# A four-layer graph network: attention tops and first-convolution flags in PSUM, nine one-hot columns in the second convolution, edge lines gathered in two stages

## The chip, the cores and the metric

The kernel runs on one core of one Trainium2 chip. The metric is device time in microseconds (us) of one execution. Engines are named as in the profile: PE (matmuls; PEld its weight loads), DVE, ACT, POOL, and SP, which issues transfers.

## The reference

6250 nodes carry 16 features. 206,250 edges are sorted by destination. Four layers follow one another, each as x + layer(relu(layernorm(x))):

```python
edge_index = jnp.stack([src, dst])
h = relu(layernorm(x)); x = x + gcn(h, edge_index, ...)           # first convolution
h = relu(layernorm(x)); x = x + nnconv(h, edge_attr_6, ...)       # second convolution
h = relu(layernorm(x)); x = x + sheaf(h, edge_index, ...)         # sheaf layer
h = relu(layernorm(x)); x = x + attention(h, edge_attr_16, ...)   # attention
```

- The first convolution sums normalised features of the source over each destination's edges: `segment_sum(h[src] * norm, dst)`.
- The second makes a 16x16 matrix of each edge's six attributes by a small network, multiplies the source's features by it, and takes the mean over the destination's edges.
- The sheaf layer makes two reflections (Householder matrices) for each edge from the features at its ends and sums messages at both ends.
- Attention makes 256 logits for each edge: `e2 = w_a * feat[src]` with `w_a = efeat @ W_attn + b_attn` as 16x16. `seg_max = segment_max(e2, dst)`, `ex = exp(e2 - seg_max[dst])`, and the output is the sum over edges of `e1 * ex / denom`, with `denom` the sum of `ex`.

## The kernel before

Edges lie on 128 partitions, 1612 in a row on each. The first three layers go through them in 62 blocks of 26 edge columns; attention groups edges of one destination in quads of four and goes through 440 quads a partition in 110 blocks of four quads. Between layers a node stage (`node_sums`) collects each destination's sum and norms. Each engine has its own program, written by hand; the engines wait for one another's semaphore counts, and the order of work on an engine is the order of its code. `At` is a block's place, `walk` unrolls some first and last blocks and loops over the rest two at a time, and `Chain` counts DVE's completions: `ch.do` counts one, `ch.to` and `ch.sync` wait for those so far, `ch.tell` waits and then signals another engine.

**Features of sources.** Part of the source rows comes by gather: POOL issues one indirect transfer for each edge column (`gather`, lines L1168, L1479, `sources` L1954, L2494). The rest comes by PE, from a table in weights: DVE or ACT makes one-hot rows (`hot`, L1191, L1610, L1687) from the source's key, PE multiplies them by the table's pieces (`summed`), DVE keeps the one wanted block of the sum (`mask`, which writes `held`), PE turns it (`picked`) and ACT copies it on (`moved`). In the first convolution this is three groups of four columns with seven one-hot rows each, all on DVE; in the second it is two groups of four columns, seven rows on ACT for one of them and four on ACT, three on DVE for the other. 14 columns of the first convolution and 18 of the second are gathered. In the second, `matrices` makes the edge's weights `w` on PE, `times` (L1711) multiplies by the features and `total` (L1719) adds up.

**Sums by destination.** A scan along each row (`scan_block`, L688) adds messages, with flags that reset it where a destination begins. In the first convolution `high_digits` (L238) and `low_digits` make one-hot digits from which PE counts degrees on the side.

**Quads and lines.** `put_quads` (L909, in the head of the second convolution, on POOL) writes where the quads begin. The node stage behind the second convolution (`quads_of_edges`, DVE) fills in which edges are in each quad, and marks void places. A line is what attention needs of the edges of a quad. For half of the quads POOL gathers lines in the sheaf layer, four each in 55 blocks (`lines` L1963), DVE puts in the void marks (`fixed` L2204) and POOL adds to the ids (`ids_of` L1971); SP stores them. The other half is gathered in attention (L2505).

**Sheaf.** Each block is done in two halves: DVE turns the gathered features (`turned`, L2257), PE and ACT make vectors from them, ACT squares, DVE multiplies (L2271) and widens (L2320), and PE sums.

**Attention.** For block `at`, DVE finds quad maxima in two steps (`larger`, L2695), carries maxima along the row (`forward` L2702) and back (`back` L2707), all in the tile `S`, subtracts them (`below` L2712), and multiplies ACT's exponentials by the messages (`product` L2719). `drop` (L2743) and `carried` (L2753) prepare the sum that enters from the block before. Between these stand the `times` (L2680) of the next block, which multiply PE's `w` in PSUM by gathered features. PE's `quad_sum` adds each quad into one of two banks `pq`, and ACT's `put_state` (L2624) copies the bank into `S`:

```python
to = pq[q % 2].rearrange("p (t c) -> p t c", t=2)
turn_wait(e, s_prod, at.of(QB, q + 1))
turn_wait(e, s_state, at.of(QB, q + 1))
for n in range(4):
    e.matmul(to, ident[:, :], X[:, q, :, n, :], start=n == 0, stop=False)
```

## Time and profile before

| | us |
|---|---|
| median of 3 runs (9060.18 to 9061.02) | 9060.25 |
| profiled execution | 9049.36 |
| its span | 9047.6 |
| first convolution, 120 to 1330 | 1210 |
| second convolution, 1470 to 3020 | 1550 |
| node stage and norm, 3020 to 3260 | 240 |
| sheaf, 3260 to 5810 | 2550 |
| attention, 5900 to 8930 | 3030 |
| busy over the span: PE / DVE / ACT / POOL | 7287.6 / 7667.6 / 4453.0 / 6665.2 |

The span is what the profiler recorded of one execution, from the first instruction to the last; the profiled execution's time has 1.8 us around it and lies 10.9 us below the median of the timed runs. The stretches of the stages were cut by hand where the lines of one stage end and those of the next begin. Busy time leaves out the issue of transfers, which on POOL takes 0.30 us ahead of each gather.

### The profile page before, as it was taken

To read this page: it belongs to the slowest core of one execution; us is meant where nothing else is said; L and a number is where in the kernel's file an instruction comes from. 1 tells how busy PE (TensorE), PEld (TensorE's weight loads), DVE (VectorE), ACT (ScalarE), POOL (GpSimd) and SP (SyncE) were. 2 spreads that over 40 slices of the span, in tenths; PEclk is the share of its full clock that TensorE was granted. 3 is DMA by queue.
4 is the path that set the end of the run, shared out by engine and by line. 5 is a ranking of instruction groups with operands and counts; after the bars stand their busy time and mean duration, and the time that the engine had idled before them with its cause. 6 is when DMAs were issued, how large, how long until landed. Compare 5 with 4: busy or idle time off the path is not lost. (4 is left out here: it accounts for less than half of the span.)

```text
span 9047.6 us, 135625 instructions
## 1 busy us (share of the span) xinstructions
PE 7287.6 (81%) x35152; PEld 4135.0 (46%) x35152; DVE 7667.6 (85%) x11882; ACT 4453.0 (49%) x7248; POOL 6665.2 (74%) x6335
## 2 busy tenths in 40 slices
PE   3778765888888258888888889578888888888884
PEld 2666653555555135555555555323333333333331
DVE  7999984777777468888888888589999999999997
ACT  4666664666666146666665556323333333333333
POOL 5777777777777577777777777377777777777774
PEclk9888886888888579999999999789999999999997
DMA  4222221112111111111111111122222222222223
GB/s 148 59 59 59 59 53 35 44 45 46 45 44 45 20 24 32 28 32 29 31 29 31 28 32 20 16 62 80 75 75 81 76 75 75 82 75 75 76 81 98
DMA packets 499695, 493.19 MB, mean 55 GB/s; under 512 B 181075, under 2 KB 396906, under 8 KB 498731
## 3 DMA queue, kind: packets, MB, share of 16 engines
q1 hardware_dynamic: 299595, 371.60, 12.2%
q0 software_dynamic: 199904, 119.78, 9.7%
q14 instruction: 171, 1.40, 0.0%
q8 instruction: 25, 0.41, 0.0%
HBM read 240.96 MB, written 249.95 MB: 54 GB/s over the span
## 5 line engine op out<-in xcount | busy, mean ns | idle before, releaser
L2494 POOL DMA_INDIRECT attn_got<-tab,attn_line x1760 | 2111.3, 1200 | 582.6 <-issue 499.4
L1954 POOL DMA_INDIRECT sheaf_got<-tab,sheaf_idx x1612 | 1710.3, 1061 | 490.0 <-issue 474.0
L2547 PE MATMUL attn_q<-attn_X,ident 128*128 128x512 f32 x3520 | 1743.8, 635 | 3.3 <-DVE attn_X L2719 1.8
L2043 PE MATMUL sheaf_acc<-sheaf_hot_hi,sheaf_wide 128*128 128x392 bf16 x6696 | 1356.9, 345 | 279.5 <-DVE sheaf_hot_hi L2246 276.1
L1479 POOL DMA_INDIRECT nnconv_got<-tab,nnconv_idx x1116 | 1082.0, 970 | 402.1 <-issue 335.1
L2547 PEld LDWEIGHTS attn_q<-attn_X,ident 128*128 128x128 f32 x3520 | 678.2, 204 | 1085.7 <-issue 1085.7
L1168 POOL DMA_INDIRECT gcn_got<-tab,gcn_idx x868 | 901.8, 1039 | 317.9 <-issue 279.2
L2680 DVE TENSOR_TENSOR attn_T<-attn_w,attn_got 128x1024 f32<-128x1024 f32 x880 | 1034.8, 1217 | 79.6 <-DVE attn_T L2712 34.1
L2043 PEld LDWEIGHTS sheaf_acc<-sheaf_hot_hi,sheaf_wide 128*128 128x128 bf16 x6696 | 656.4, 106 | 816.5 <-issue 488.4
L2624 ACT COPY attn_S<-attn_q 128x512 f32<-128x512 f32 x440 | 255.9, 582 | 1559.8 <-PE attn_q L2556 1559.8
L1257 PE MATMUL gcn_acc<-gcn_hot,pieces 128*128 128x512 f32 x2604 | 752.3, 448 | 268.7 <-DVE gcn_hot L1191 267.2
L1191 DVE SCALAR_TENSOR_TENSOR gcn_hot<-gcn_key,key_of,gcn_one 128x512 fp32r<-128x512 f16 x1302 | 872.3, 740 | 4.6 <-DMA gcn_blk<-src_blk 4.6
L2538 PE MATMUL attn_w<-src_hi 32*128 32x512 f32 x3520 | 588.4, 741 | 342.8 <-DVE attn_T L2680 341.9
L1257 PEld LDWEIGHTS gcn_acc<-gcn_hot,pieces 128*128 128x128 f32 x2604 | 554.3, 219 | 402.5 <-issue 280.7
L1711 DVE TENSOR_TENSOR nnconv_prod<-nnconv_w,nnconv_got 128x1024 f32<-128x1024 f32 x434 | 490.3, 1142 | 271.4 <-PE nnconv_w L1514 270.7
L2043 PE MATMUL sheaf_acc<-sheaf_hot_act,sheaf_wide 128*128 128x392 bf16 x2976 | 613.6, 345 | 0.0
L2105 ACT ACTIVATE sheaf_zT<-sheaf_z,sheaf_b 128x832 f32<-128x832 f32 x248 | 223.2, 951 | 722.3 <-PE sheaf_z L1995 722.3
L2712 DVE SCALAR_TENSOR_TENSOR attn_T<-attn_T,attn_S 128x1024 f32<-128x1024 f32 x440 | 536.0, 1218 | 17.3 <-DVE src_lo L2743 16.6
L1514 PE MATMUL nnconv_w<-nnconv_W,nnconv_tT 64*128 64x256 f32 x3224 | 537.3, 462 | 4.4 <-DVE nnconv_prod L1711 4.4
L1529 PE MATMUL nnconv_acc<-nnconv_hot,pieces 128*128 128x512 f32 x1736 | 529.5, 465 | 11.7 <-ACT nnconv_hot L1610 11.7
L2719 DVE SCALAR_TENSOR_TENSOR attn_X<-attn_T,attn_X 128x1024 f32<-128x1024 f32 x440 | 525.8, 1215 | 1.2 <-ACT attn_X L2610 1.2
L2246 DVE TENSOR_SCALAR sheaf_hot_hi<-sheaf_number,src_hi 128x784 bf16<-128x784 f16 x1116 | 477.9, 428 | 42.8 <-PE sheaf_acc L2043 26.2
(503 smaller groups left out, 13356.6 us busy)
## 6 DMA issues: line engine op xcount, KB each, us to landing
sums<-attn_S SPq DMA_DIRECT2D x110, 1024.0 KB, 4.2
tops<-attn_S SPq DMA_DIRECT2D x110, 512.0 KB, 3.0
attn_got<-tab,attn_line POOLq DMA_INDIRECT x1760, 2.5
sheaf_got<-tab,sheaf_idx POOLq DMA_INDIRECT x1612, 2.5
gcn_key<-src_key SPq DMA_DIRECT2D x62, 384.0 KB, 3.7
gcn_blk<-src_blk SPq DMA_DIRECT2D x62, 384.0 KB, 4.2
nnconv_got<-tab,nnconv_idx POOLq DMA_INDIRECT x1116
nnconv_key<-src_key SPq DMA_DIRECT2D x62, 256.0 KB
```

The source lines that it names most:

```text
L1168: e.indirect_dma_start(out=got[at.b][:, j, :], out_offset=None, in_=tab[0], in_offset=indices(idx[at.b], j)).then_inc(s_got[at.b], 16)
L1191: hit = e.scalar_tensor_tensor(out=hot[q][:, n, :], in0=key[at.b][:, g, :], scalar=key_of[:, n:n + 1], in1=pone[:, :], op0=ALU.is_equal, o ...
L1257: mm = e.matmul(pacc[q][:, :], pieces[:, part, n * NBLK:(n + 1) * NBLK, :].rearrange("p b f -> p (b f)"), hot[q][:, n, :], start=n + part ...
L1479: e.indirect_dma_start(out=got[at.b][:, j, :], out_offset=None, in_=tab[1], in_offset=indices(idx[at.b], j)).then_inc(s_got_of[part][at.b] ...
L1514: mm = [e.matmul(to[:, t * 512 + (j - 2 * g) * 256:t * 512 + (j - 2 * g + 1) * 256], tT[at.b][t * H1:(t + 1) * H1, j * P:(j + 1) * P], W2[ ...
L1954: e.indirect_dma_start(out=got[at.b][:, j, D:D + T2], out_offset=None, in_=tab[2], in_offset=indices(idx[at.b], j)).then_inc(s_got[half][a ...
L2043: mm = e.matmul(pacc[k][:, 0:HH], wide[at.b][half][:, part, col, :], hot[:, k * HH:(k + 1) * HH], start=False, stop=False, skip_group_chec ...
L2494: e.indirect_dma_start(out=got[at.b][:, 4 * q + n, :], out_offset=None, in_=tab[3], in_offset=indices(ids[:, q, n, :], D + 2)).then_inc(s_ ...
L2538: e.matmul(pw[n // 2][:, n % 2 * 512:(n % 2 + 1) * 512], efT[at.b][n * RW:(n + 1) * RW, q, :], Wc[n * RW:(n + 1) * RW, :], start=True, sto ...
L2547: e.matmul(to, ident[:, :], X[:, q, :, n, :], start=n == 0, stop=False)
L2680: e.tensor_tensor(T[at.b][:, q, :, 2 * half:2 * half + 2, :].rearrange("p t n (i o) -> p n t i o", o=D), pw[half].rearrange("p (n t i o) - ...
L2712: return ch.do(e.scalar_tensor_tensor(out=Tb[:, q, 0, :, :], in0=Tb[:, q, 0, :, :], scalar=1.0, in1=Sb[:, q, None, 0:CH].to_broadcast([P, ...
```

## The change

First convolution: the scan's flags, and a table of digits for `high_digits`, lie in PSUM; the ones that the hot rows read shrink to 128 columns; the seventh one-hot row of each group goes from DVE to ACT, as Square and Relu (`last_row`). Second convolution: three groups of three columns in place of two of four, so 17 columns are gathered; rows on ACT are 7, 5 and 0 of seven, the rest on DVE; masks stand ahead of the totals. From block 14 on, two lines a block are gathered there too, 96 in all, with index and marks on ACT and ids on DVE. `quads_of_edges` moves from the node stage into blocks 10 to 13, in pieces, and `void_src` goes. Sheaf: two lines a block in all 62 blocks in place of four in 55; the ids are added on DVE. Attention: the tops lie in PSUM (`ptop`), which ACT copies out (`tops_out`); `pq` shrinks to one bank; `times` come in halves between the steps of the maxima, and some waits of DVE for its own completions go.

```diff
@@ first convolution
-            runT, msgT, flags = ([sbl(f"{n}{b}", [P, D, J + 1]) for b in range(2)] for n in ("runT", "msgT", "flags"))
+            runT, msgT = ([sbl(f"{n}{b}", [P, D, J + 1]) for b in range(2)] for n in ("runT", "msgT"))
+            pflag = [ps(f"gcn_flag{b}", [P, 512], banks) for b in range(2)]
+            flags = [t[:, 0:D * (J + 1)].rearrange("p (f j) -> p f j", f=D) for t in pflag]
+            high = pone[:, P:P + C]
+            BY_DVE = NC - 1
-                        for n in range(NC):
-                            hit = e.scalar_tensor_tensor(out=hot[q][:, n, :], in0=key[at.b][:, g, :], scalar=key_of[:, n:n + 1],
-                                                         in1=pone[:, :], op0=ALU.is_equal, op1=ALU.mult)
+                        for n in range(BY_DVE):
+                            hit = e.scalar_tensor_tensor(out=hot[q][:, n, :].rearrange("p (j m) -> p j m", j=GW),
...
+                                                         in1=pone[:, None, 0:P].to_broadcast([P, GW, P]), op0=ALU.is_equal, op1=ALU.mult)
+                    def last_row(at, g):
+
+                        q = (at.b * GP + g) % 2
+                        if g == 0:
+                            e.wait_ge(s_rows[at.b], at.half(32, 32))
+                        e.wait_ge(s_acc, at.of(GP, g + 1))
+                        e.activation(hot[q][:, NC - 1, :], key[at.b][:, g, :], ACT.Square,
+                                     bias=key_neg[:, NC - 1:NC]).then_inc(s_apart, 1)
+                        e.wait_ge(s_apart, at.of(GP, g + 1))
+                        e.activation(hot[q][:, NC - 1, :], hot[q].bitcast(F32)[:, NC - 1, :], ACT.Relu, scale=-1.0,
+                                     bias=ones[:, 0:1]).then_inc(s_last, 1)
@@ second convolution
-        GN = 2
-        BY_ACT = (NC, 4)
+        GN, GC = 3, 3
+        BY_ACT = (NC, 5, 0)
+                    def lines(ln):
+
+                        turn_wait(e, s_at, ln.of(1, 1))
+                        if ln.k >= 2:
+                            turn_wait(e, s_lst[ln.b], ln.half(16, 0))
+                        for q in range(NP2):
+                            e.indirect_dma_start(out=line[ln.b][:, q, :, :].rearrange("p n f -> p (n f)"), out_offset=None,
+                                                 in_=a["lines"], in_offset=indices(line_at[ln.b], q)).then_inc(s_ln[ln.b], 16)
...
+                        if at.k >= KL:
+                            lines(at.plus(-KL))
...
+                            if more and pair[0] in (2, 4):
+                                mask(at.plus(1), pair[0] // 2)
                             for g in pair:
                                 added[g] = total(at, g)
-                            if more and pair[0] == 2:
-                                mask(at.plus(1), 1)
+                            if at.k == KL - 3 and pair[0] == 0:
+                                quads_across()
+                            if at.k == KL - 2 and pair[0] == 0:
+                                quads_carried()
+                            if more and pair[0] == 0:
+                                chosen(at.plus(1), 2)
...
+                        if at.k == KL - 4:
+                            quads_within()
+                        if at.k == KL - 2:
+                            quads_of_edges()
+                        if at.k == KL - 1:
+                            quads_joined()
+                        if at.k >= KL:
+                            ids_of(at.plus(-KL))
@@ sheaf, POOL
                     def step(at):
                         sources(at, 0)
-                        if 0 < at.k <= NBL:
-                            ids_of(at.plus(-1))
                         sources(at, 1)
-                        if at.k < NBL:
-                            lines(at)
+                        lines(at)
@@ attention
-            pq = [ps(f"attn_q{q}", [P, 512], banks) for q in range(2)]
+            pq = ps("attn_q", [P, 512], banks)
+            ptop = ps("attn_tops", [P, QB * CH], banks).rearrange("p (q c) -> p q c", q=QB)
-                        turn_wait(e, s_state, at.of(QB, q + 1))
+                        turn_wait(e, s_state, at.of(QB, q + 2))
+                    def tops_out(at):
+
+                        e.wait_ge(s_sub, at.of(QB, QB))
+                        e.copy(S[at.b][:, :, 0:CH], ptop).then_inc(s_copied, 1)
-                                out=Sb[:, q, 0:CH], in0=Sb[:, q + 1, 0:CH], scalar=apart_q[:, bass.ds(at.of(QB, q + 1), 1)],
+                                out=ptop[:, q, :], in0=ptop[:, q + 1, :], scalar=apart_q[:, bass.ds(at.of(QB, q + 1), 1)],
-                        ch.tell(s_top)
+                        e.scalar_tensor_tensor(out=drop[:, :], in0=So[:, QB - 1, 0:CH], scalar=1.0, in1=ptop[:, 0, :],
+                                               op0=ALU.mult, op1=ALU.subtract).then_inc(s_top, 1)
                         below(0)
-                        ch.tell(s_sub)
```

Three places show what moves. On ACT in the first convolution, from the store of one block's run (`gcn_run`) on, there stood before:

```order
L1328 COPY gcn_run<-gcn_runT 128x416
L1306 COPY gcn_msgT<-gcn_sel 128x4x16
L692 COPY gcn_flags<-same 128x16x26
L1335 ACTIVATE gcn_apart<-iota_f,src_lo 128x128 x8
L1306 COPY gcn_msgT<-gcn_sel 128x4x16
L1335 ACTIVATE gcn_apart<-iota_f,src_lo 128x128 x9
```

and now stands:

```order
L1251 COPY gcn_run<-gcn_runT 128x416
L1218 ACTIVATE gcn_hot<-gcn_key,key_neg 128x512
L1221 ACTIVATE gcn_hot<-gcn_hot,ones 128x512
L1235 COPY gcn_msgT<-gcn_got 128x14x16
L1239 COPY gcn_idx<-srci 128x14
L1229 COPY gcn_msgT<-gcn_sel 128x4x16
L695 COPY gcn_flag<-same 128x16x26
L1258 ACTIVATE gcn_apart<-iota_f,src_lo 128x128 x8
L1218 ACTIVATE gcn_hot<-gcn_key,key_neg 128x512
L1221 ACTIVATE gcn_hot<-gcn_hot,ones 128x512
L1229 COPY gcn_msgT<-gcn_sel 128x4x16
L1258 ACTIVATE gcn_apart<-iota_f,src_lo 128x128 x9
```

A Square and a Relu (`gcn_hot`) come ahead of each copy of a group's sums (`gcn_msgT<-gcn_sel`, which is `moved`), and the copies of gathered rows and of the next indices come to the start of the step.

On DVE in the second convolution, in the products (`nnconv_prod`, which is `times`) and totals (`nnconv_msgT`) of one block, there stood before:

```order
L1711 TENSOR_TENSOR nnconv_prod<-nnconv_w,nnconv_got 128x1024 x2
L1719 TENSOR_REDUCE nnconv_msgT<-nnconv_prod 128x4x16 x2
L1711 TENSOR_TENSOR nnconv_prod<-nnconv_w,nnconv_got 128x1024 x2
L1719 TENSOR_REDUCE nnconv_msgT<-nnconv_prod 128x4x16 x2
L1695 SCALAR_TENSOR_TENSOR nnconv_held<-nnconv_blk,blk_of,nnconv_acc 128x512
L1711 TENSOR_TENSOR nnconv_prod<-nnconv_w,nnconv_got 128x1024 x2
L1719 TENSOR_REDUCE nnconv_msgT<-nnconv_prod 128x4x16 x2
L1687 TENSOR_SCALAR nnconv_hot<-nnconv_key,key_of 128x512 x3
```

and now stands:

```order
L1724 TENSOR_TENSOR nnconv_prod<-nnconv_w,nnconv_got 128x1024 x2
L1732 TENSOR_REDUCE nnconv_msgT<-nnconv_prod 128x4x16 x2
L1700 TENSOR_SCALAR nnconv_hot<-nnconv_key,key_of 128x384 x7
L1724 TENSOR_TENSOR nnconv_prod<-nnconv_w,nnconv_got 128x1024 x2
L1708 SCALAR_TENSOR_TENSOR nnconv_held<-nnconv_blk,blk_of,nnconv_acc 128x384
L1732 TENSOR_REDUCE nnconv_msgT<-nnconv_prod 128x4x16 x2
L1724 TENSOR_TENSOR nnconv_prod<-nnconv_w,nnconv_got 128x1024 x2
L1708 SCALAR_TENSOR_TENSOR nnconv_held<-nnconv_blk,blk_of,nnconv_acc 128x384
L1732 TENSOR_REDUCE nnconv_msgT<-nnconv_prod 128x4x16 x2
L1700 TENSOR_SCALAR nnconv_hot<-nnconv_key,key_of 128x384 x2
```

The mask of the next block's group (`nnconv_held`) has moved ahead of two totals, there is one mask more, and nine one-hot rows of 384 columns stand in place of three of 512.

On DVE in attention, from the quad maxima (`attn_two`) of one block on, there stood before:

```order
L2695 SCALAR_TENSOR_TENSOR attn_two<-attn_T 128x2048
L2695 SCALAR_TENSOR_TENSOR attn_S<-attn_two 128x4x256
L2702 SCALAR_TENSOR_TENSOR attn_S<-attn_S,apart_q 128x256
L2691 SCALAR_TENSOR_TENSOR attn_line<-void,attn_line 128x8
L2680 TENSOR_TENSOR attn_T<-attn_w,attn_got 128x2x2x256 x2
L2702 SCALAR_TENSOR_TENSOR attn_S<-attn_S,apart_q 128x256 x3
L2707 SCALAR_TENSOR_TENSOR attn_S<-attn_S,apart_q 128x256
L2712 SCALAR_TENSOR_TENSOR attn_T<-attn_T,attn_S 128x1024
```

and now stands:

```order
L2798 SCALAR_TENSOR_TENSOR attn_two<-attn_T 128x1024 x2
L2783 TENSOR_TENSOR attn_T<-attn_w,attn_got 128x2x2x256
L2798 SCALAR_TENSOR_TENSOR attn_S<-attn_two 128x4x256
L2794 SCALAR_TENSOR_TENSOR attn_line<-void,attn_line 128x8
L2805 SCALAR_TENSOR_TENSOR attn_S<-attn_S,apart_q 128x256
L2783 TENSOR_TENSOR attn_T<-attn_w,attn_got 128x2x2x256
L2805 SCALAR_TENSOR_TENSOR attn_S<-attn_S,apart_q 128x256
L2783 TENSOR_TENSOR attn_T<-attn_w,attn_got 128x2x2x256
L2805 SCALAR_TENSOR_TENSOR attn_S<-attn_S,apart_q 128x256
L2805 SCALAR_TENSOR_TENSOR attn_tops<-attn_S,apart_q 128x256
L2811 SCALAR_TENSOR_TENSOR attn_tops<-attn_tops,apart_q,attn_S 128x256
L2816 SCALAR_TENSOR_TENSOR attn_T<-attn_T,attn_tops 128x1024
```

Halves of the next block's products (`attn_T<-attn_w`) stand between `larger` and the steps of `forward`, and from the last of these on the tops are written to and read from PSUM (`attn_tops`).

## Rows read from the trace of the kernel before

**Rows 1.** Windows, attention: us, busy of PE, PEld, DVE, ACT, POOL; clock; DMA.

```profile
5900.00:8930.00 3030.00, 2681.64 (x8343) 1054.14 (x8343) 2863.43 (x3079) 970.19 (x1865) 2323.18 (x1970) 0.93 0.26 76
```

**Rows 2.** Timeline of DVE, first convolution: start, us, operation, xcount [idle before <-releaser].

```profile
700.68 1.06 DVE L688 TENSOR_TENSOR_SCAN gcn_runT<-gcn_flags,gcn_msgT 128x432 f32<-128x432 f32 x1
...
702.71 4.69 DVE L1191 SCALAR_TENSOR_TENSOR gcn_hot<-gcn_key,key_of,gcn_one 128x512 fp32r<-128x512 f16 x7
...
707.32 1.48 DVE L238 TENSOR_TENSOR gcn_digits<-iota_b,src_hi 128x1274 bf16<-128x1274 bf16 x1
...
719.73 1.06 DVE L688 TENSOR_TENSOR_SCAN gcn_runT<-gcn_flags,gcn_msgT 128x432 f32<-128x432 f32 x1
```

**Rows 3.** Timeline of POOL, the same stretch.

```profile
700.93 1.57 POOL L1168 DMA_INDIRECT gcn_got<-tab,gcn_idx  x1 [0.30 <-issue]
...
707.84 1.78 POOL L1168 DMA_INDIRECT gcn_got<-tab,gcn_idx  x1 [0.30 <-issue]
...
711.18 0.95 POOL L1168 DMA_INDIRECT gcn_got<-tab,gcn_idx  x1 [0.30 <-issue]
```

**Rows 4.** Waits of ACT, first convolution: us in total, times, longest.

```profile
ACT gcn_msgT L1306 <- PE gcn_sel L1269: 391.4, 125, 18.5
```

**Rows 5.** Timeline of POOL, second convolution, the first gathers of three blocks.

```profile
1668.49 1.01 POOL L1479 DMA_INDIRECT nnconv_got<-tab,nnconv_idx  x1 [0.99 <-POOL nnconv_idx L1473]
...
2432.74 0.97 POOL L1479 DMA_INDIRECT nnconv_got<-tab,nnconv_idx  x1 [0.96 <-POOL nnconv_idx L1473]
...
2955.82 0.97 POOL L1479 DMA_INDIRECT nnconv_got<-tab,nnconv_idx  x1 [1.85 <-DVE nnconv_prod L1711]
```

**Rows 6.** Waits of DVE and of PE, second convolution.

```profile
DVE nnconv_prod L1711 <- PE nnconv_w L1514: 270.7, 131, 3.3
...
PE nnconv_sel L1542 <- DVE nnconv_held L1695: 187.5, 99, 2.7
```

**Rows 7.** Timeline of DVE, sheaf, two transposes in the last blocks.

```profile
5579.34 0.60 DVE L2257 STREAM_TRANSPOSE sheaf_gT<-sheaf_got 128x416 f32<-128x416 f32 x1
...
5599.70 0.60 DVE L2257 STREAM_TRANSPOSE sheaf_gT<-sheaf_got 128x416 f32<-128x416 f32 x1
```

**Rows 8.** Waits of DVE, sheaf.

```profile
DVE sheaf_line L2204 <- issue: 82.2, 24, 3.6
```

**Rows 9.** Waits of DVE, attention.

```profile
DVE attn_T L2680 <- DVE attn_T L2712: 34.1, 109, 0.3
...
DVE attn_T L2712 <- DVE src_lo L2743: 16.6, 105, 0.2
```

**Rows 10.** Groups of POOL, attention: busy us, mean ns | idle before <-releasers.

```profile
L2494 POOL DMA_INDIRECT attn_got<-tab,attn_line x1752 | 2103.7, 1201 | 580.1 <-issue 497.0 <-DMA attn_line<-quad_lines 58.0 <-DMA attn_got<-tab,attn_line 16.5
```

**Rows 11.** Groups by form of ACT, second convolution.

```profile
L1606 ACT ACTIVATE nnconv_hot<-nnconv_key,key_neg 128x512 fp32r<-128x512 f16 x671 | 424.1, 715 | 0.0
```

**Rows 12.** Groups by form of PEld (weight loads), second convolution.

```profile
L1529 PEld LDWEIGHTS nnconv_acc<-nnconv_hot,pieces 128*128 128x128 f32 x1730 | 384.5, 229 | 151.6 <-issue 62.8
```

**Rows 13.** Groups by form of POOL, node stage behind the second convolution.

```profile
L880 POOL DMA_INDIRECT agg<-runs,last_edge x49 | 52.1, 1063 | 14.9 <-issue 14.9
```

**Rows 14.** Timeline of ACT, attention.

```profile
7514.40 0.59 ACT L2624 COPY attn_S<-attn_q 128x512 f32<-128x512 f32 x1 [3.52 <-PE attn_q L2556]
```

**Rows 15.** Timeline of PE, attention.

```profile
7514.29 1.14 PE L2538 MATMUL attn_w<-src_hi 32*128 32x512 f32 x8
...
7529.07 2.09 PE L2538 MATMUL attn_w<-src_hi 32*128 32x512 f32 x8 [3.15 <-DVE attn_T L2680]
```

**Rows 16.** Timeline of DVE, attention.

```profile
7515.69 2.34 DVE L2680 TENSOR_TENSOR attn_T<-attn_w,attn_got 128x1024 f32<-128x1024 f32 x2
```

**Rows 17.** Groups by form of DVE, attention.

```profile
L2680 DVE TENSOR_TENSOR attn_T<-attn_w,attn_got 128x1024 f32<-128x1024 f32 x880 | 1034.8, 1217 | 79.6 <-DVE attn_T L2712 34.1 <-DVE attn_X L2719 29.2 <-PE attn_w L2538 8.8
...
L2712 DVE SCALAR_TENSOR_TENSOR attn_T<-attn_T,attn_S 128x1024 f32<-128x1024 f32 x440 | 536.0, 1218 | 17.3 <-DVE src_lo L2743 16.6
...
L2753 DVE SCALAR_TENSOR_TENSOR src_lo<-attn_S,src_lo 128x512 f32<-128x512 f32 x110 | 75.4, 686 | 0.0
```

More of the change, by code:

```diff
@@ L1359, in _ @@
                     flagged(At(0))
+                    for g in range(GP):
+                        last_row(At(0), g)
                     for g in range(GP - 1):
+                        last_row(At(1), g)
                         moved(At(0), g)
@@ L1574, in _ @@
                     summed(At(1), 0)
-                    walk(e, NB, step)
+                    walk(e, NB, step, head=KL)
                 @block.scalar
@@ L1719, in total, with quads_within @@
                         return ch.do(e.tensor_reduce(by_edge(msgT[at.b][:, :, 1 + 4 * g:1 + 4 * g + n]), prod[g % 3][:, 0:n, :, :], AX.X, ALU.add))
+                    def quads_within():
+                        ch.do(e.memset(nil[:, :], 0.0))
+                        ch.do(e.memset(moved_on[:, 0:1], 0.0))
+                        e.wait_ge(s_pool, 2)
+                        ch.do(e.tensor_copy(edge_f[:, :], edge_i[:, :]))
+                        ch.do(e.tensor_copy(f4[:, :], lane_i[:, :]))
+                        e.wait_ge(s_ld, 32)
+                        flags = begun[:, :, 3]
+                        ch.do(e.tensor_scalar(goes[:, :], flags, -1.0, 1.0, ALU.mult, ALU.add))
+                        ch.do(e.tensor_reduce(f1[:, :], flags, AX.X, ALU.add))
+                        ch.sync()
+                        for f in range(3):
+                            ch.do(e.tensor_tensor_scan(fill[:, f, :], goes[:, :], begun[:, :, f], 0.0, ALU.mult, ALU.add))
+                        ch.do(e.tensor_scalar(f1[:, :], f1[:, :], 0.5, None, ALU.is_lt))
+                        ch.sync()
+                        ch.do(e.tensor_copy(ends[:, :], fill[:, :, LQ - 1]))
+                        ch.do(e.tensor_scalar(diag[:, :], ident[:, :], f1[:, 0:1], None, ALU.mult))
+                        ch.tell(s_end)
@@ L1721, in step, with ids_of @@
+                    def ids_of(ln):
+                        e.wait_ge(s_ln[ln.b], ln.half(16 * NP2, 16 * NP2))
+                        ids = line[ln.b].bitcast(I32)[:, :, :, D + 2]
+                        e.scalar_tensor_tensor(out=ids, in0=void[:, bass.ds(ln.of(QB, 0), NP2), :], scalar=float(NP), in1=ids,
+                                               op0=ALU.mult, op1=ALU.add).then_inc(s_ids, 1)
                     def step(at):
@@ L2669, in _, with times @@
                     e.sem_inc(s_t, 2)
-                    def times(at, q):
-                        if q == 0 and at.k >= 2:
+                    def times(at, q, halves=(0, 1)):
+                        if q == 0 and at.k >= 2 and 0 in halves:
                             e.wait_ge(s_prod, at.of(QB, -QB))
-                        if q % 2 == 0:
+                        if q % 2 == 0 and 0 in halves:
                             e.wait_ge(s_got[q // 2][at.b], at.half(16 * EH, 16 * EH))
-                        for half in range(2):
+                        for half in halves:
                             for n in (2 * half, 2 * half + 1):
```

425 lines of the change are left out of this document (228 added, 197 removed).

## The prediction

> **What bounds the kernel now.** I read the table of windows by stage first; its row for attention [rows 1] shows DVE busy for 2863 of 3030 us and POOL for 2323, to which POOL's issue gaps come. Neither is the one full engine of the program: the stages have different limits, so each is read by itself, in its timelines and then its waits, for what ends last there.
>
> First convolution, 62 blocks. In DVE's timeline the scans of two blocks start at 700.68 and 719.73 [rows 2]: 19.05 us a block. DVE fills it with 21 one-hot rows (seven in 4.69, a new one every 0.66), three masks, `high_digits` (1.48) and the scan (1.06). POOL needs as long: 14 gathers of 0.95 with 0.30 between, but the one that starts in `high_digits` takes 1.78 and the one that starts in the scan 1.57 [rows 3]; both end about 0.8 after the DVE instruction does. Those two read both inputs from SBUF. The hot rows, whose ones lie in PSUM, delay no gather. ACT waits 391 us for PE's sums, 6.3 a block [rows 4]: it has room.
>
> Second convolution, 62 blocks. POOL starts block 8 at 1668.49, block 40 at 2432.74 and block 61 at 2955.82 [rows 5]. To block 40 that is 23.9 a block, the gaps before a block being only those behind its index copy; after it 24.9, with waits of about 2 for DVE's products. POOL falls back in the head, where it also puts out quad rows, regains its lead in 32 blocks and then waits. So the consumers bound, at 24.9: DVE waits 270.7 for PE's `w`, PE 187.5 for DVE's masks [rows 6], of which `mask(1)` stands behind two totals.
>
> Sheaf, 62 blocks of 41 us (2550 / 62). POOL's 26 sources and 4 lines take 37.5 even undisturbed and its gathers never stop in the loop, which looks like a bound. Against it: the last seven blocks gather no lines, and there two halves still start 20.4 apart, 5579.34 and 5599.70 [rows 7]. Also DVE stops 24 times for 3.4 at the line copy, once a turn of the loop, for nothing that the profile shows [rows 8].
>
> Attention, 110 blocks of 27.5 (3030 / 110). DVE waits mostly for its own dependent steps, 0.16 to 0.32 each [rows 9]. POOL's gathers average 1.20 instead of 0.95 [rows 10].
>
> **The change part by part.**
>
> First convolution. DVE loses three rows, 2.0: 17.1. POOL loses the two delays, 0.83 + 0.62: 14 x 1.25 = 17.5. ACT gains three rows, each a Square of 128x512, 0.72 in the second convolution [rows 11], and a Relu of the same 512 elements that depends on it and that I price alike: 1.4 a row, 4.2 a block, on 19.05 - 6.3 = 12.8: 17.0. Three engines within half a microsecond, with ACT's rows queued ahead of `moved`, will not interlock perfectly. I take 18.0: -1.05 x 62 = **-65**. Ends: 17.5 (-96), and ACT taking it all back (0).
>
> Second convolution. POOL gives up one of 18 gathers a block (-1.25) and takes two line gathers (+2.5) in the last 48: about 22.7 before block 14 and 25.2 after it, and perhaps 0.2 for nine DVE rows in place of three. DVE turns 3 rows and 2 masks into 9 and 3 shorter ones: at 0.66 for 512 columns [rows 2] and 0.5 for 384, 5 x 0.66 = 3.3 becomes 12 x 0.5 = 6.0, at most +2.7. It also takes over the edge-of-quad work, some 40 instructions on 440 columns: at half of a scan's 1.06, 20 us in four blocks. PE goes from 28 products to 42: no more columns to speak of, but 14 more weight loads of 0.229 [rows 12], so 0 to +3.2; I take +1.3. What pays: masks come before totals, so PE's 3.0 a block for them shrinks, and DVE's wait for `w` behind it. I let both cancel. POOL's 25.2 to 25.4 against 24.9 then eats its regained lead over 48 blocks without becoming the bound for long. With the 20 us, partly in DVE's waits for PE, and a little for POOL at the end: **+20**. Ends: 0 (POOL's own sum: -62 x 1.25 + 96 x 1.25 = +43, less the 2 us waits of 20 blocks) and +100 (consumers +1.3 a block).
>
> Node stage behind it. Its 49 gathers are the path: 52.1 + 14.9 [rows 13]. At 0.945 they would take 46.3; the edge-of-quad instructions beside them go: **-4**, between -6 and 0.
>
> Sheaf. POOL loses two lines and two small additions a block, 3.0 of 41; DVE exchanges a copy for an addition of the same size. By the tail POOL is not what ends last: **-5**. Ends 0, and -105 if 1.7 of POOL's 3.0 a block came off (the other 1.3 standing for the stop of 3.4 in every second block).
>
> Attention. On DVE the wait after `below(0)` goes (0.3), that after `drop` (0.16), `forward` steps lie between halves of `times` (0.2), `larger` no longer waits for all of `two` (0.1), and `carried` tells without a wait: 0.7 to 1.0 a block, cover included. POOL loses what `below`, `back` and part of `forward` held: of 16 x 0.26 = 4.1 a block I expect 1.6 to go, which leaves POOL below DVE. In the way stands PE. `quad_sum(1)` writes the one bank that `put_state(0)` still reads, so it waits for that copy (0.59 [rows 14]) and two hand-overs, 0.8. The `w` behind it now ends at 7514.29 + 1.14 = 7515.43, and DVE begins with it at 7515.69 [rows 15, 16]: a slack of 0.26. So up to half a microsecond comes back as a wait there. Later in the block PE waits 3.15 for DVE, and the eight matmuls behind that wait take 2.09 instead of 1.14; so the 0.8 has room only in the 3.15. Half of the pure gain of 1.0 lost would be -55, none lost -110; I take -0.7 x 110 = **-77**, ends 0 and -115.
>
> Does a PSUM operand cost DVE more? `times`, with one input in PSUM, takes 1.217 and `below`, all SBUF, 1.218 for the same 1024 elements [rows 17]. A hot row of 512 with its ones in PSUM takes 4.69 - 6 x 0.66 = 0.73, `carried` of 512 in SBUF 0.686. So 0 to 0.05 an instruction; I take 0. The Trainium skill, "VectorE: DVE Perf Modes", section "The TRN2 errata — SBUF-src ops pay a fixed extra latency per instruction", lists a fixed 58 cycles for SBUF and 120 for PSUM, which makes an estimate of 0.065 us for each of nine instructions that move in an attention block: by that the sum would lose 64 us. The rows of 1024 elements do not agree with it, those of 512 nearly do.
>
> Sum: -65 + 20 - 4 - 5 - 77 = -131. The profiled execution took 9049.4, its span 9047.6; so 8918. The median of the three runs lies 10.9 above that execution: **8929 us**.
>
> **Rivals.**
> - *ACT becomes the first convolution's bound*, 19 a block: Square and Relu stand between PE's sum and `moved` in its order. For it the thin margin, against it 6.3 of idle for 4.2 of work. No gain there: 8994. Chance 0.13.
> - *The single bank costs attention its gain*: DVE waits for `w` as long as PE for the copy, -0.1 x 110 instead of -77: 8995. For it the slack of 0.26, against it the idle 3.15. Chance 0.14.
> - *PSUM operands are dearer*: nine instructions at 0.05 in 110 blocks, 50, and two in 62 blocks, 6: 8985. Chance 0.10.
> - *Sheaf was bound by POOL after all*: -105 instead of -5: 8829. For it POOL's unbroken row, against it the tail. Chance 0.10.
> - *The second convolution's added work lies on its path*, the slower side: PE and DVE already wait for each other, so +1.3 and +2.7 add up: 62 x 4.0 = 248 instead of 20: 9157. It decides from (131 + 20) / 62 = 2.4 a block on. Against it the 3.0 a block that PE now waits for masks. Chance 0.08.
>
> **How the numbers follow.** The forecast has 0.45, the rivals 0.55. Sheaf's -105 and the slower case are left out (0.18). The rest spans 8845, with the first convolution and attention at their best ends (8929 - 31 - 38, and some from sheaf), to 9040, with one rival of the middle group and the second convolution at +65. As the forecast's own range I see 8875 to 8985. 0.2% is 18 us, about what a measurement of this kernel can tell from no change: faster 0.83, same 0.07, slower 0.10.
>
> **What would show it.** First convolution: scans 17.5 to 18.3 apart, gathers all near 0.95, ACT with little idle time. Second: gathers 25.2 a block at the end, PE's wait for masks below 100 in all, blocks near 25. Sheaf: POOL waiting for DVE, blocks still near 41. Attention: gathers near 1.10, a new wait of PE for `attn_S` of about 0.8 a block, DVE waiting 0.2 to 0.5 for `w`. The prediction is wrong if the second convolution's blocks pass 26, if the first stays at 19, or if DVE's wait for `w` in attention reaches 1 a block.

## The result and the profile after

The changed kernel takes **9259.57 us** (median of 4 runs, 9256.27 to 9261.85), the kernel before 9060.22: a ratio of 1.022, 95% interval 1.0203 to 1.0238. It is slower by 199 us, where 131 less was forecast, and outside the predicted range.

The profiled execution has a span of 9260.1 us against 9047.6. Here is where the 212.5 us between them lie. A stage's length is taken on VectorE, from the first start to the last of its one-hot rows, its products, its transposes and its maxima (`gcn_hot`, `nnconv_prod`, `sheaf_gT`, `attn_two`), from the listing of one tile's instructions:

| stage | before | after | difference | forecast |
|---|---|---|---|---|
| first convolution | 1177.8 | 1081.6 | -96 | -65 |
| from it to the second | 185.0 | 197.2 | +12 | 0 |
| second convolution | 1523.6 | 1752.0 | +228 | +20 |
| node stage | 211.7 | 207.0 | -5 | -4 |
| sheaf | 2517.3 | 2589.7 | +72 | -5 |
| attention | 2978.9 | 2978.0 | -1 | -77 |

The rows add up to 210; the rest lies ahead of the first stage, between the sheaf layer and attention, and behind attention.

The table of windows after, one row a stage; the last answers to [rows 1] (us; busy time and count on PE, PEld, DVE, ACT, POOL; granted clock of PE, where 1.00 is the upper of its two levels, 2.4 GHz, and 0.50 the lower, 1.2 GHz; DMA):

```profile
120.00:1230.00 1110.00, 921.20 (x5678) 774.13 (x5678) 1020.68 (x1493) 1044.09 (x2455) 825.75 (x868) 0.90 0.25 62
1385.00:3160.00 1775.00, 1381.19 (x7910) 1108.71 (x7909) 1359.70 (x1885) 943.23 (x1686) 1131.86 (x1212) 0.84 0.19 47
3365.00:5960.00 2595.00, 2291.37 (x13713) 1368.08 (x13714) 2138.63 (x5252) 1508.88 (x1646) 1827.20 (x1713) 0.90 0.14 23
6110.00:9140.00 3030.00, 2655.97 (x8341) 1021.64 (x8341) 2833.65 (x3189) 1071.69 (x1975) 2135.42 (x1971) 0.95 0.26 76
```

No engine is full in the second convolution: the longest, PE and DVE, are busy for 1381 and 1360 of 1775 us. They wait for each other, and for longer than in [rows 6]:

```profile
PE nnconv_sel L1518 <- DVE nnconv_held L1708: 362.3, 175, 6.0
DVE nnconv_prod L1724 <- PE nnconv_w L1489: 351.9, 131, 5.9
```

In the sheaf layer DVE still waits for nothing that the profile shows where it did in [rows 8], and in a second place, both 24 times, once a turn of the loop:

```profile
DVE sheaf_line L2300 <- issue: 80.1, 24, 3.5
DVE sheaf_prod L2369 <- issue: 33.6, 24, 1.6
```

In attention DVE is busy 30 us less and POOL's gathers are shorter (1099 ns against 1201 in [rows 10]), but the time stays; the group of `times`, whose wait for PE's `w` was 8.8 in [rows 17], and PE's wait for the copy out of the one bank:

```profile
L2783 DVE TENSOR_TENSOR attn_T<-attn_w,attn_got 128x1024 f32<-128x1024 f32 x880 | 1054.4, 1220 | 151.7 <-PE attn_w L2637 116.5 <-DVE attn_X L2823 29.5 <-DMA attn_got<-tab,attn_line 5.6
```
```profile
PE attn_q L2646 <- ACT attn_S L2726: 91.8, 114, 0.9
```

### The profile page after: what moved, and what is told of

It reads as the page before. It is cut to its first block and busy times, and to the rows that moved or that the text cites. A ratio compares the mean times of both kernels' runs of the same rounds, so it can differ in the third digit from the quotient of the medians.

```text
span 9260.1 us, 138201 instructions
## 1 busy us (share of the span) xinstructions
PE 7358.3 (79%) x36144; PEld 4337.8 (47%) x36144; DVE 7636.0 (82%) x12309; ACT 4727.1 (51%) x8012; POOL 6324.6 (68%) x6163
## 5 line engine op out<-in xcount | busy, mean ns | idle before, releaser
L2593 POOL DMA_INDIRECT attn_got<-tab,attn_line x1760 | 1933.9, 1099 | 770.5 <-issue 502.6
L2140 PE MATMUL sheaf_acc<-sheaf_hot_hi,sheaf_wide 128*128 128x392 bf16 x6696 | 1412.0, 355 | 286.4 <-DVE sheaf_hot_hi L2344 286.4
L1452 POOL DMA_INDIRECT nnconv_got<-tab,nnconv_idx x1054 | 1018.8, 967 | 386.1 <-issue 297.0
L2646 PEld LDWEIGHTS attn_q<-attn_X,ident 128*128 128x128 f32 x3520 | 651.7, 198 | 1191.7 <-issue 1191.7
L2783 DVE TENSOR_TENSOR attn_T<-attn_w,attn_got 128x1024 f32<-128x1024 f32 x880 | 1054.4, 1220 | 151.7 <-PE attn_w L2637 116.5
L1073 POOL DMA_INDIRECT gcn_got<-tab,gcn_idx x868 | 825.8, 951 | 303.8 <-issue 276.2
L1097 DVE SCALAR_TENSOR_TENSOR gcn_hot<-gcn_key,key_of,gcn_one 128x512 fp32r<-128x512 f16 x1116 | 750.4, 743 | 4.0 <-DMA gcn_blk<-src_blk 4.0
L1505 PE MATMUL nnconv_acc<-nnconv_hot,pieces 128*128 128x384 f32 x2604 | 700.0, 438 | 16.5 <-ACT nnconv_hot L1600 9.9
L2140 PE MATMUL sheaf_acc<-sheaf_hot_act,sheaf_wide 128*128 128x392 bf16 x2976 | 656.6, 363 | 0.0
L1505 PEld LDWEIGHTS nnconv_acc<-nnconv_hot,pieces 128*128 128x128 f32 x2604 | 643.7, 264 | 18.6 <-issue 18.6
L2816 DVE SCALAR_TENSOR_TENSOR attn_T<-attn_T,attn_tops 128x1024 f32<-128x1024 f32 x440 | 533.0, 1211 | 0.0
```

Source lines behind the costliest of these rows:

```text
L1073: e.indirect_dma_start(out=got[at.b][:, j, :], out_offset=None, in_=tab[0], in_offset=indices(idx[at.b], j)).then_inc(s_got[at.b], 16)
L1097: hit = e.scalar_tensor_tensor(out=hot[q][:, n, :].rearrange("p (j m) -> p j m", j=GW), in0=key[at.b][:, g, :].rearrange("p (j m) -> p j m ...
L1452: e.indirect_dma_start(out=got[at.b][:, j, :], out_offset=None, in_=tab[1], in_offset=indices(idx[at.b], j)).then_inc(s_got_of[part][at.b] ...
L1505: mm = e.matmul(pacc[:, 0:GC * P], pieces[:, part, n * NBLK:(n + 1) * NBLK, :].rearrange("p b f -> p (b f)"), hot[q][:, n, :], start=n + p ...
L2140: mm = e.matmul(pacc[k][:, 0:HH], wide[at.b][half][:, part, col, :], hot[:, k * HH:(k + 1) * HH], start=False, stop=False, skip_group_chec ...
L2593: e.indirect_dma_start(out=got[at.b][:, 4 * q + n, :], out_offset=None, in_=tab[3], in_offset=indices(ids[:, q, n, :], D + 2)).then_inc(s_ ...
```

## The experiments

The chips on which they ran timed the kernel before at 9048.8 to 9068.8 us (medians), so single times are read beside the kernel before on the same chip, and small differences by the stage's length. That has a spread too: with its code as it was before, sheaf takes 2509.0 to 2522.7 us in five runs, attention 2978.9 to 2991.5 in three.

### Second convolution: the masks' place

The timelines of DVE and of PE in the kernel after, block 30 or so (start, us, operation, xcount, idle before):

```profile
2304.93 2.34 DVE L1732 TENSOR_REDUCE nnconv_msgT<-nnconv_prod 128x64 f32<-128x1024 f32 x2
2307.18 2.41 DVE L1700 TENSOR_SCALAR nnconv_hot<-nnconv_key,key_of 128x384 fp32r<-128x384 f16 x7
2309.51 2.34 DVE L1724 TENSOR_TENSOR nnconv_prod<-nnconv_w,nnconv_got 128x1024 f32<-128x1024 f32 x2
2311.78 0.60 DVE L1708 SCALAR_TENSOR_TENSOR nnconv_held<-nnconv_blk,blk_of,nnconv_acc 128x384 f32<-128x384 f16 x1
2312.30 2.33 DVE L1732 TENSOR_REDUCE nnconv_msgT<-nnconv_prod 128x64 f32<-128x1024 f32 x2
2318.90 1.23 DVE L1724 TENSOR_TENSOR nnconv_prod<-nnconv_w,nnconv_got 128x1024 f32<-128x1024 f32 x1 [4.26 <-PE nnconv_w L1489]
```
```profile
2303.71 2.73 PE L1505 MATMUL nnconv_acc<-nnconv_hot,pieces 128*128 128x384 f32 x14
...
2308.32 1.14 PE L1489 MATMUL nnconv_w<-nnconv_W,nnconv_tT 64*128 64x256 f32 x8
2312.68 1.12 PE L1518 MATMUL nnconv_sel<-nnconv_pick,nnconv_held 128*128 128x32 f32 x6 [3.21 <-DVE nnconv_held L1708]
2313.61 4.00 PE L1505 MATMUL nnconv_acc<-nnconv_hot,pieces 128*128 128x384 f32 x14
```

PE's sum is complete at 2306.4. By then DVE is in two totals, and its program has seven one-hot rows and two products before the mask, which starts 5.3 us after the sum, at 2311.78. PE waits 3.21, its next sum takes 4.00 instead of 2.73, and DVE, which ran ahead to the mask, waits 4.26 for the `w` behind that sum. Each engine's delay is the other's next wait. The wait also costs clock: in the windows of PE the granted clock is 1.00 during the first sum (2303.7 to 2306.4), and 0.50 from 2313.5 to 2315.5 in the sum behind the wait, which is what makes the same 14 matmuls longer.

**Masks early.** In `step` of DVE (changed kernel), the mask that PE waits for goes ahead of what does not need it:

```diff
-                            if more and pair[0] in (2, 4):
-                                mask(at.plus(1), pair[0] // 2)
                             for g in pair:
                                 added[g] = total(at, g)
...
+                            if more and pair[0] in (0, 2):
+                                mask(at.plus(1), pair[0] // 2 + 1)
                             if more and pair[0] == 0:
                                 chosen(at.plus(1), 2)
```

> The changed kernel with two of VectorE's masks in the second convolution put earlier: the second mask behind the first pair's sums and ahead of its seven one-hot rows, the third behind the second pair's sums and ahead of the next products. Theory (order: the masks stand behind products and rows that do not need them, and TensorE waits for them): TensorE's wait for the mask falls from 358.7 us to under 120, the later blocks from 28.2 to 24.7 to 25.7 us, the stage by 120 to 190 us, the time to 9070 to 9140. Rival (the ninth columns' work, the loads and the line gathers fill the block): the waits move to other names, the blocks stay at 27 or more, the time stays at 9210 to 9260.

Measured: 9035.7 us beside 9056.0 for the kernel before; the stage takes 1530.0 instead of 1752.0, a larger gain than I expected. DVE's wait for `w` nearly goes, and one for PE's sum, 17.8 in the changed kernel, comes:

```profile
PE nnconv_sel L1518 <- DVE nnconv_held L1708: 187.3, 60, 8.4
DVE nnconv_prod L1724 <- PE nnconv_w L1489: 50.1, 60, 5.1
DVE nnconv_held L1708 <- PE nnconv_acc L1505: 90.6, 60, 7.2
```

PE's wait did not fall below the 120 us that I expected: it is now one stop of about 3 us a block. That stop is not free: the sum behind it is again at the lower clock (granted 0.59 from 2202.4 to 2206.6) and takes 4.1 to 4.2 us, and DVE waits for it, 60 times and 90.6 us in all. But DVE waits for PE for 141 us in all, where it waited 370 in the changed kernel, and is busy for 1365 of the 1565 us between 1385 and 2950. The stage's 222 us come from the order alone, with the same instructions; how much of them is the clock (0.89 in this stage, 0.84 before the masks moved) and how much the waits themselves, no run separates. The rival falls.

**No lines.** The changed kernel, masks late, without the line gathers, index copies, marks and ids of this stage.

> The changed kernel, its masks where the change put them, without the line gathers of the second convolution and what goes with them on the other engines; half of the quads keep lines of zeros, so only the second convolution is read. Theory (the masks' place is the cost, the lines a little beside it): later blocks 27.2 to 27.6 us instead of 28.2, the stage 30 to 45 us shorter. Rival (the lines are the cost): blocks of 24.5 to 25.5 us, the stage 130 us shorter or more.

Measured: 1726.1 us, 26 less than the changed kernel and a little less of a gain than I expected: the lines cost little where the masks set the pace. (Its time was 9154.7, because the sheaf stage fell too, to 2508.8; see below.)

**Nine columns alone.** The kernel before with the three groups of three and the masks early; lines and quads' setup stay where they were.

> The kernel before with the nine columns in three groups in the second convolution alone, VectorE's masks early, and neither the edge lines nor the quads' setup in it. Theory (the columns themselves are a gain, their order took it): blocks of 23.0 to 23.7 us instead of 24.65, 60 to 100 us less, time 8950 to 9000. Rival (the second one-hot rows on VectorE and the third mask eat what eight or nine gathers less give): blocks of 24.4 to 25.0, time 9040 to 9080.

Measured: 8996.3 beside 9055.1; the stage takes 1465.9, 58 less than before. Blocks take 23.3 to 24.7 us, a little more than I expected, but the columns are a gain. Beside the run with masks early, 1530.0, lines and quads' setup in this stage cost 64 us together.

### First convolution: which part pays

Tiles lie in one of two memories on the chip, SBUF or PSUM; PE's sums go to PSUM.

**First convolution alone**, put into the kernel before.

> The kernel before with the change's first convolution alone. Theory (each stage's part stands by itself): first convolution's block 17.5 us, 95 us less, time 8955 to 8975. Rival (part of the stage's gain comes back where the next stages wait for transfers that start earlier): 8985 to 9030.

Measured: 8958.0 beside 9056.0, the stage 1079.6: this part stands by itself. **The seventh row back on VectorE** (changed kernel):

```diff
-            BY_DVE = NC - 1
+            BY_DVE = NC
```

> The changed kernel with the first convolution's seventh one-hot row back on VectorE. Theory (VectorE's sum of 19.05 us bounded the block of before, and the row's 2 us a block is the gain): blocks of 18.8 to 19.2 us instead of 17.5, 75 to 105 us more, time 9335 to 9365. Rival (the flags in the other memory, which make GpSimd's gathers cheaper, are the gain): blocks of 17.5 to 18.0, 0 to 30 us more.

**Flags and block numbers back in SBUF** (changed kernel):

```diff
-            flags = [t[:, 0:D * (J + 1)].rearrange("p (f j) -> p f j", f=D) for t in pflag]
-            high = pone[:, P:P + C]
+            flags = [sbl(f"flags{b}", [P, D, J + 1]) for b in range(2)]
+            high = sbl("high", [P, C])[:, :]
```

> The changed kernel with the first convolution's flags and the row of block numbers in SBUF as before, the seventh row on ScalarE. Theory (the seventh row on ScalarE is nearly all of the stage's gain): first convolution 0 to 30 us longer than the changed kernel's 1081 us. Rival (the flags in PSUM take VectorE out of the way of GpSimd's gathers, which bounded the block): 50 to 95 us longer.

Measured (VectorE is the profile's DVE): 1157.4 us with the row on VectorE and 1144.6 with the flags in SBUF, against 1081.6 with both parts and 1177.8 with neither. Each part alone gives 20 or 33 us, both together 96. Neither of my two expectations held as a whole: the row's holds in its size (76 back), but its time, 9232.6, does not, as the sheaf stage fell with it (see below); and the flags are not a small thing beside it (63 back, the rival's size; time 9325.7). They are two bounds of nearly the same length, and the stage keeps the one that is left: with the row on VectorE DVE is busy for 1072.8 of the 1100 us from 120 to 1220, with the flags in SBUF for 976.0, and there POOL's gathers (837.8) and their issue (257.5) fill the time. The listings of POOL's gathers show the second bound (min/median/max in ns), first of the changed kernel, then with the flags in SBUF:

```profile
L1073 POOL DMA_INDIRECT gcn_got<-tab,gcn_idx x868: 946/952/968, 124.2 to 1226.4; - x174
```
```profile
L1072 POOL DMA_INDIRECT gcn_got<-tab,gcn_idx x868: 947/952/2317, 123.8 to 1292.9; - x174
```

With the second inputs of the scan and of `high_digits` in PSUM no gather is longer than 968 ns; with both inputs in SBUF the longest takes 2317, 102 of the 868 take over 1200, and all together take 894.8 us instead of 825.8: 69 more, on a stage that is 63 longer. The Trainium skill says in "SBUF — State Buffer", section "Who interferes with whom", that a VectorE instruction with two inputs in SBUF contends with a GpSimd instruction that reads SBUF; the gathers take their indices from a tile there, and these two runs agree with it.

### Sheaf: what the 72 us are

My first theory was pace: POOL, with four line gathers a block before, held the halves at 19.4 us, and with two it no longer does. Two runs were to show it from both sides.

**Two spare line gathers** more in each block of the changed kernel, into tiles that nobody reads:

```diff
...
+                        for q in range(NP2):
+                            e.indirect_dma_start(out=spare[at.b][:, q, :, :].rearrange("p n f -> p (n f)"), out_offset=None,
+                                                 in_=a["lines"], in_offset=indices(edges_of, q)).then_inc(s_sp[at.b], 16)
...
```

> The changed kernel with two more line gathers a block in the sheaf layer, into tiles that nobody reads, so that GpSimd has its four line gathers a block again. Theory (GpSimd's gathers paced the halves of before; without them VectorE's and ScalarE's hand-overs meet badly): sheaf blocks of 40.8 to 41.4 us instead of 42.6, stage 70 to 100 us shorter, time 9160 to 9190. Rival (VectorE's two operations for the lines' ids and the stop at the loop's turn are the cost): blocks stay at 42.4 to 42.8 or get longer, time 9250 or more.

**Two lines less** in each block of the kernel before.

> The kernel before with two of the four line gathers a block left out of the sheaf layer; half of the quads keep lines of zeros, so attention works on other indices and only the sheaf stage is read. Theory (pacing): sheaf blocks grow from 41.0 to about 42.6 us, the stage by 70 to 100 us. Rival (GpSimd's gathers bound the block): blocks of 39 us or less, the stage 100 us shorter or more.

Measured: 2586.1 us with the spare gathers (2589.7 without), and 2505.0 with two lines less in the kernel before (2517.3). The theory falls on both sides. The rival of the second run falls as well: two gathers of about 1.25 less a block, 155 us of POOL's work, took at most 12 us off, about the spread of this stage, so POOL is no bound of it.

What spoke instead were two runs that had not touched the sheaf layer. With the seventh row on VectorE its stage took 2497.3, without lines in the second convolution 2508.8. Both changed the number of instructions ahead of the loop in VectorE's program, and with it the stops: both gone in the first (first instruction 2010), the second gone in the other (1985). **The program moved** tests that alone: the changed kernel with 18 tiny memsets at the stage's start, which put the loop's first instruction at VectorE's number 2010, where it is with the seventh row, instead of 1992.

```diff
                     ch.tell(s_ready)
+                    for n in range(18):
+                        ch.do(e.memset(prod[:, n % 13, n // 13, 0:1], 0.0))
```

> The changed kernel with 18 tiny memsets ahead of the sheaf loop in VectorE's program, so that the loop's first instruction is VectorE's number 2010, as in the run with the seventh row on VectorE, instead of 1992. Theory (the sheaf layer's 72 us are stops in which VectorE waits for instructions, and these hang on where its loop lies in its program): both stops at the loop's turn go, sheaf blocks 40.8 to 41.1 us, stage 80 to 95 us shorter, time 9160 to 9185. Rival (the stage's time hangs on ScalarE's program or on what the stage meets when it starts): blocks stay at 42.67, time 9245 or more.

Measured: 9174.9, the stage 2505.6, 84 us less for 18 instructions more. DVE's list of waits has neither stop any longer. The page's rows of the instruction queue, of the changed kernel and of this one (packets, MB):

```profile
q14 instruction: 184, 1.50, 0.1%
```
```profile
q14 instruction: 63, 0.52, 0.0%
```

121 packets less, five for each of 24 turns. Between 3600 and 5500 us, inside the loop, the changed kernel has 111 of them, the moved one none, and the kernel before, with one stop, 110: the packets go with the loop, but not with the second stop. I read it so: with the loop at 1992 VectorE has to fetch in each turn of its 370 instructions, with the loop at 2010 it does not. The transposes show what that did to a turn of two blocks. Without stops its four halves take 20.3 to 20.6 us (medians). With the first stop alone, in the kernel before, the half that holds it takes 22.2, but two others 19.4 and 19.8: the loop catches up. With both, 23.4, 20.5, 20.5 and 20.9: it does not. Why not is open; no run has the second stop alone.

**48 and 176 memsets** in the kernel of all parts that pay (below) were to show which places are good.

> The parts that pay, together, with 48 tiny memsets ahead of the sheaf loop, so that the loop begins at VectorE's instruction 1370 instead of 1322. 2010, where no stop was seen, is 1370 and five times 128. If the place that matters repeats every 128 instructions, the stop of 3.5 us at the loop's turn goes and the sheaf stage takes 2495 to 2508 us instead of 2516. If it repeats every 256, this place lies half a period off 2010 and the stop can stay. Rival (the place in the whole program or another engine's decides): the stop stays here and with 176.

> The same with 176 memsets: the loop begins at VectorE's instruction 1498; 2010 is 1498 and twice 256. If the place that matters repeats every 128 or every 256 instructions, the stop goes, sheaf stage 2495 to 2508 us. If the stop goes here and stays with 48, the period is 256 (or another divisor of 512 above 128). Rival: the stop stays in both.

Measured: the stop is gone in both, blocks 40.96 us instead of 41.20, the stage 2507.5 and 2511.4 instead of 2516.1, packets of that queue 53 instead of 172. 1370, 1498 and 2010 lie 90 behind a multiple of 128; the places with a stop (1265, 1282, 1285, 1322, 1339, 1985, 1992) lie 113, 2, 5, 42, 59, 65 and 72 behind one. A period of 128 fits all of them, and so would 64 or 32. The times, 8842.5 and 8842.1, are no better than without memsets: taking out a stop that the loop catches up with takes 5 to 9 us off the stage, which is within its spread.

### Attention: the one bank

**One bank in the kernel before**, nothing else:

```diff
-            pq = [ps(f"attn_q{q}", [P, 512], banks) for q in range(2)]
+            pq = [ps("attn_q", [P, 512], banks)] * 2
...
-                        turn_wait(e, s_state, at.of(QB, q + 1))
+                        turn_wait(e, s_state, at.of(QB, q + 2))
...
-                        else:
-                            turn_wait(e, s_state, at.of(QB, q + 2))
```

> The kernel before with one accumulator bank for the quad sums instead of two, nothing else. Theory (the one bank ate what the rest of the attention change gave): attention 70 to 115 us longer, time 9130 to 9175, VectorE's wait for w of the second quad near 1 us a block. Rival (the bank costs nothing here and the tops in the other memory cost what they saved): within 15 us of 9060.

Measured: 9230.0 beside 9056.0; attention 3150.7, 172 us longer. That is more than the 110 us of one wait of 1 us a block: DVE waits for `w` 159 times and 189.6 us in all, where the kernel before has 8.8 [rows 17] and the changed kernel 116.5. If the parts add up, the rest of the change gives back what this bank takes; no run has that rest with two banks.

**The second quad's products early** in the changed kernel: PE's `matrices(nxt, 1)` goes between the matmuls of `quad_sum(prev, 1)`.

```diff
-                            if at.k > 0:
-                                quad_sum(prev, q)
+                            early = q == 1 and 0 < at.k < NBQ - 1
+                            if at.k > 0:
+                                quad_sum(prev, q, (lambda: matrices(nxt, 1)) if early else None)
...
-                            if at.k < NBQ - 1:
+                            if at.k < NBQ - 1 and not early:
```

> The changed kernel with TensorE's products for the next block's second quad put between the matmuls of the previous block's second quad sum instead of behind all of it. Theory (the one accumulator bank makes the quad sum start late, and the products stand behind it): VectorE's wait for w falls from 116.5 us to under 40, attention gets 70 to 112 us shorter, the time is 9145 to 9190. Rival (TensorE's own chain through the one bank sets the block): the wait for w is replaced by one for the state or the next quad's w, the time stays within 20 us of 9259.

Measured: 9196.8; attention 2919.7, 58 us less. Its waits:

```profile
PE attn_q L2646 <- ACT attn_S L2727: 175.4, 223, 0.9
DVE attn_T L2784 <- PE attn_w L2637: 6.5, 5, 2.3
```

PE waits for the bank twice a block now and DVE hardly for PE: the wait has moved to the engine that has room. The gain is below the 70 that I expected. Of the 110 us that go, 34 come back as waits of DVE that the one for `w` had covered (21.0 for ACT's exponentials, 13.3 for its copies of the state). Of the other 18, DVE's own busy time takes 11 (2818 us in the stage instead of 2807); the rest stays open.

### The parts that pay

First convolution as changed; second convolution with nine columns and masks early; attention as changed with the products early; lines and quads' setup where they were before.

> The parts that pay, together: first convolution as changed, second convolution with nine columns and the masks early, attention as changed with the second quad's products early; edge lines and the quads' setup where they were before. Theory (the parts add up): 98 and 60 to 100 and 55 to 65 us less than before, time 8790 to 8845. Rival (the sheaf loop falls on a place in VectorE's program with a second stop, about 72 us, or attention's gain depends on the lines' other order): 8865 to 8910.

Measured: **8836.6 us** (median of 4 runs), a ratio to the kernel before of 0.9757, 95% interval 0.9741 to 0.9773. The stages take 1079.2, 1466.5, 2516.1 and 2920.3: the sum of the parts.

## Why the prediction was wrong

- **First convolution: right in mechanism, too small.** Three bounds within half a microsecond was the right reading, and the two that I named on DVE and POOL are there, as the two runs that undo one of them show. The term was mis-sized in "will not interlock perfectly. I take 18.0": the scans lie 17.52 apart ((1229.8 - 161.1) / 61), the best end of the range. They interlock: POOL's own sum, 14 gathers of 0.952 with 0.30 between, is 17.5, and in the loop it waits for next to nothing else. ACT's wait for PE's sums [rows 4] has shrunk from 391 to 0.9 us, so ACT was nearly a bound too, but at 17.5 and not at its rival's 19.
- **Second convolution: the step "What pays: masks come before totals" failed.** I saw that a mask moves ahead of the totals of its own pair, and did not ask what else lies between it and PE's sum. That sum now comes a set of products earlier, and seven new rows stand ahead of the mask. The rival that let the added work lie on the path named 9157 and a block 4.0 longer; the block was 3.7 longer (28.33 against 24.64, from the scans), but not for the added work: the same work runs in 24.79 with the masks early. The sum had the order only as a gain, which it let cancel with the added work; it had no price for the order as a cost. That the rival's number is near is luck. The block passes the 26 that the prediction named as a sign that it is wrong.
- **Node stage: right** (-5): its 49 gathers take 46.3 us, as the prediction had them. The +12 ahead of the second convolution was in no term; it comes with the first convolution alone too (191.6 there), in part.
- **Sheaf: "By the tail POOL is not what ends last" was right, and -5 still wrong.** The 72 us are not of the stage's change: the 3.4 us stop that I had listed [rows 8] and taken as fixed hangs on where VectorE's loop lies in its program, and the change moved it from 1282 to 1992. Moving it by 18 takes 84 us off. (The prediction's end of -105 has a slip that changes nothing: a stop of 3.4 in every second block is 1.7 a block, which leaves 1.3 of POOL's 3.0, or -81.)
- **Attention: the rival of the single bank came true**, -1 against its -11. The step that failed is "up to half a microsecond comes back as a wait", the 0.8 less the slack of 0.26 us between `w` and DVE's demand for it. DVE waits about 1.0 each time, the third sign of being wrong that the prediction named. Measured from the first quad's products (medians of 90 blocks), `w` for the second quad was complete after 6.34 us before and is after 7.37: 1.03 later and not 0.8. And the slack was not free: DVE starts 0.13 behind the end of `w` even when it waits, and the median distance before was 0.16. DVE itself asks no earlier (6.5 in both). What the change was to free came: DVE is busy 30 us less, its waits after `below` (34.1) and `drop` (16.6) [rows 9] are gone, and the gathers take the 1.10 that was expected.
- **PSUM operands: right at nothing.** `below`, now with the tops in PSUM, takes 1211 ns for 1024 elements where it took 1218:

```profile
L2816 DVE SCALAR_TENSOR_TENSOR attn_T<-attn_T,attn_tops 128x1024 f32<-128x1024 f32 x440 | 533.0, 1211 | 0.0
```

## What to carry to other kernels

When a producer's work is moved forward, move the consumer's answer with it: count what stands in the consumer's program between the moment its input is there and the instruction that the producer waits for, since a gain in work (58 us here) can be lost several times over (222) in an order in which two engines wait in turn. Where two bounds are nearly equal, test a part of the change only together with its partner: each alone was worth 20 or 33 us, both 96. And a stage that the edit hardly touches can move by 3% through the length of the program ahead of its loop: list the waits that nothing releases, and shift the program, before explaining such a difference by the work.

## What was unexpected in the hardware

By the packets of the instruction queue inside the loop (111 or none between 3600 and 5500 us), VectorE's loop of 370 instructions is fetched anew in every turn or not at all, depending on its place: 184 packets in the whole run and two stops a turn (up to 3.5 and 1.6 us) at number 1992, 63 packets and none at 2010; the good places seen are equal modulo 128. One stop a turn already goes with the fetches (before: 171 packets). The Trainium skill, "Runtime: NRT & Kernel Launch", section "Instruction fetch mechanics", says that a taken branch to a target outside of the two pages held forces a fetch; the stops at the loop's turn agree with it. The two pages of 256 instructions that it gives do not fit the places, wherever the pages begin: if a loop of 372 fits into two of them from 1370 and from 1498 but not from 1322, then one of 370 fits from 1992 too. What is kept, and why the second stop is not caught up with, stays open.
